# Four portions of x matmuls in place of five, in a graph aggregation kernel on one core

## What is computed

```python
def _L0_gnn_ref(feat_src, review_feat, edge_w, node_w, review_w, src_idx, dst_idx):
    h = feat_src @ node_w.T
    rf = review_feat @ review_w.T
    m = (h[src_idx] + rf) * edge_w
    return jax.ops.segment_sum(m, dst_idx, num_segments=N_DST)
x = _layernorm(x + _L0_gnn_ref(x, edge_attr_64, edge_weight1, ...), axis=-1)
```

## Time and profile before

| | us |
|---|---|
| median of 2 runs | 2188.48 |
| lowest, highest | 2188.12, 2188.84 |
| the profiled execution's own time | 2191.23 |
| its span, first to last instruction | 2189.4 |
| TensorE / VectorE / ScalarE / GpSimd busy | 1842.9 / 1854.2 / 1432.4 / 1582.9 |

### The profile page before, as it was taken

One profiled execution on the slowest core, in us unless ns is written; L12 is line 12 of the kernel. 1 busy time (PEld: TensorE's weight loads), 2 busy tenths in 40 slices (PEclk: granted clock), 3 DMA queues, 4 the chain that ended last, 5 costly groups with the idle time before them and its releaser, 6 DMA issues.

```text
span 2189.4 us, 95528 instructions
## 1 busy us (share of the span) xinstructions
PE 1842.9 (84%) x35999; PEld 1621.5 (74%) x36000; DVE 1854.2 (85%) x5664; ACT 1432.4 (65%) x2705; POOL 1582.9 (72%) x1539
## 2 busy tenths in 40 slices
PE   1669798979898989888898899889988997989984
PEld 1558687868787878777787788778877886878874
DVE  3859797979798989888898899789978897979974
ACT  1547675767676766766676667566766775767744
POOL 3777777777777777777777777777777777777501
PEclk8679898989999999989999999899989998989997
DMA  7223333333343333333333334333433343333302
GB/s 144 50 64 84 82 83 75 85 75 84 81 88 80 87 80 88 80 85 73 87 83 84 72 86 86 81 74 84 88 76 73 83 92 75 81 76 86 69 4 59
DMA packets 480122, 173.28 MB, mean 79 GB/s; under 512 B 443549, under 2 KB 455397, under 8 KB 479445
## 3 DMA queue, kind: packets, MB, share of 16 engines
q1 hardware_dynamic: 426791, 111.57, 23.8%
q0 software_dynamic: 49632, 51.95, 10.7%
q10 hardware_dynamic: 3218, 3.20, 0.7%
HBM read 163.39 MB, written 3.20 MB: 76 GB/s over the span
## 4 chain that ended last, share of the span: by engine, by line
POOL 63%; issue 20%; PE 7%; DVE 6%; DMA 2%; ACT 1%; DVEq 0%; POOLq 0%; ACTq 0%; SPq 0%
POOL rows L541 60%; PE x_ps L1493 3%; PE count_ps L1480 3%; POOL work L567 2%; DVE hot_lo L865 2%; DVE hot_key L864 1%; DMA counts<-dst 1%; POOL dst_row L559 1%; PE unit_ps L1405 1%; DMA dst_row<-dst,row_i 1%; ACT x_tab L1361 1%; DVE work L1000 0%; ACT counts L1283 0%; DVE x_tab L1020 0%; DVE x_tab L1008 0%
## 5 line engine op out<-in xcount | busy, mean ns | idle before, releaser
L541 POOL DMA_INDIRECT rows<-x,g_src_cols x1440 | 1496.1, 1039 | 443.4 <-issue 438.4
L1283 ACT ACTIVATE counts<-count_ps 128x588 f32<-128x588 f32 (+1 forms) x1192 | 836.0, 746 | 617.5 <-PE count_ps L1480 615.0
L1480 PE MATMUL count_ps<-hot_key,hot_lo 128*128 128x294 f32 x4552 | 863.5, 325 | 242.3 <-DVE hot_lo L865 177.4
L865 DVE SCALAR_TENSOR_TENSOR hot_lo<-count,cols 128x256 fp32r<-128x256 f16 x2276 | 1051.8, 477 | 1.0
L1480 PEld LDWEIGHTS count_ps<-hot_key,hot_lo 128*128 128x128 f32 x4552 | 664.2, 195 | 347.3 <-issue 170.5
L1493 PE MATMUL x_ps<-counts,x_tab 128*64 128x63 f32 x21364 | 789.7, 227 | 19.4 <-DVE sums L779 18.4
L1493 PEld LDWEIGHTS x_ps<-counts,x_tab 128*64 128x64 f32 x21364 | 715.7, 140 | 77.0 <-issue 26.1
L864 DVE TENSOR_SCALAR hot_key<-count,cols 128x294 fp32r<-128x294 f16 x1734 | 668.0, 385 | 71.7 <-PE count_ps L1480 60.1
L1240 ACT ACTIVATE hot_key<-far_key,all_ones 128x294 fp32r<-128x294 f16 x542 | 293.6, 542 | 17.6
L1238 ACT ACTIVATE far_key<-count,neg_key 128x294 f16<-128x294 f16 x542 | 284.7, 525 | 0.1
L1405 PE MATMUL unit_ps<-rows,g_hot 128*32 128x64 f32 x5760 | 120.1, 245 | 0.0
(11 more groups left out here) (199 smaller groups left out, 768.5 us busy)
## 6 DMA issues: line engine op xcount, KB each, us to landing
rows<-edge_attr SPq DMA_DIRECT2D x196, 512.0 KB
rows<-x,g_src_cols POOLq DMA_INDIRECT x1440
out<-x_tab SPq DMA_DIRECT2D x12, 256.0 KB
counts<-dst SPq DMA_DIRECT2D x1, 848.0 KB
a_stage<-dst SPq DMA_DIRECT2D x17, 48.0 KB
a_stage_w<-edge_weight SPq DMA_DIRECT2D x17, 48.0 KB
g_stage<-src SPq DMA_DIRECT2D x18, 40.0 KB
g_stage<-dst SPq DMA_DIRECT2D x18, 40.0 KB
```

The lines of the kernel that those rows point to most:

```text
L541: pool.indirect_dma_start(out=g_x[:, i, t, :], out_offset=None, in_=x, in_offset=bass.IndirectOffsetOnAxis(ap=g_src_cols[at.p][:, k:k + 1] ...
L865: dve.scalar_tensor_tensor(hot_lo[h][:, :, :], count16[:, 0:P].unsqueeze(1).to_broadcast([P, 2, P]), cols_[:, LO, j:j + 1], cols_[:, W_LOW ...
L1283: act.activation(to, count_ps[(g + e) % 2][:, 0:n, 0:KEYS].rearrange("p a (h d) -> p a h d", d=D), ACT.Copy).then_inc(counts_read, 1)
L1480: done = pe.matmul(count_ps[(g + e) % 2][:, k % 2, 0:KEYS], hot_lo[h][:, i, :], hot_key[h][:, :], start=(i == 0), stop=(i == 1))
```

## The change

The constants place four portions at k = 5, 10, 15 and 20 instead of five at 4, 8, 12, 16 and 20. The portions hold 24, 25, 24 and 25 x matmuls (before: 19, 20, 19, 20 and 20). The sums and products of the units move with them. On VectorE three positions move: `add_g` with the next `make_g_slot_hot` from 15 to 16, `make_a_hot` from 18 to 21, and `add_a` with the next `make_a_slot_hot` from 24 to 26. `make_g_hot` stays at 9. No instruction is added or removed, and ScalarE's, GpSimd's and SyncE's orders stay as they are.

```diff
-PORTIONS_AT = (4, 8, 12, 16, 20)
-SUM_G, MULTIPLY_G, SUM_A, MULTIPLY_A, TURN = 4, 8, 12, 16, 8
+PORTIONS_AT = (5, 10, 15, 20)
+SUM_G, MULTIPLY_G, SUM_A, MULTIPLY_A, TURN = 5, 10, 15, 20, 8
...
-                        if k == 15 and has_g:
+                        if k == 16 and has_g:
                             add_g(at, g)
                             if later_g:
                                 make_g_slot_hot(*next_unit(at, g, GATHERED))
-                        if k == 18 and later_a:
+                        if k == 21 and later_a:
                             make_a_hot(*next_unit(at, g, SUMMED))
                         if k == 22 and g == 1 and not last:
                             find_runs(at.r + 1)
-                        if k == 24 and has_a:
+                        if k == 26 and has_a:
                             add_a(at, g)
```

## The result

The changed kernel takes 2214.76 us (2213.83 to 2215.70, two runs) against 2188.48: the ratio is 1.011, with a 95% interval of 1.009 to 1.014. That is slower, by 26.3 us, and within the 2% that count as the same here. The forecast was 2198.5, in a range of 2189 to 2226: 10 us more were expected, 26 came, so the time lies in the range and 16 us above its centre. The profiled executions took 2191.23 and 2213.83 us and so differ by 22.6; the rest lies in how each stands to its median. Spans are 2189.4 and 2212.1.

What follows compares the result with a forecast made beforehand. GpSimd's 84 gathers, 113.2 us a round, were taken as the bound; two rounds of steps, 224.5 us, fit its 226.4, so 16 rounds cost nothing. The end adds 10 us: 2188.5 to 2198.5 us, range 2189 to 2226.

Steps and rivals of the forecast that it cites:

- What bounds: GpSimd, going from gather to gather without a stop, sets the period for 16 rounds: 84 gathers, 113.2 us a round.
- Five windows in a row: Between portions, a third pair waits for the first pair's evacuation: 0.45 us at windows 8, 14 and 18, 1.35 a step.
- Window 4: TensorE waits there for ScalarE's evacuation of windows 0 and 1, delayed by keys: 1.19 us a step.
- The plain step: TensorE's own work of 15.35 us plus waits of 1.35 and 1.19: 17.9 us, 2.1 more than before.
- The 16 rounds: Two rounds of steps, 224.5 us, still fit GpSimd's 226.4; line 809's wait falls from 134 to 50 to 80 us.
- Rival B: Steps outgrow GpSimd, over about 18.2 us on average; line 809's wait vanishes; 2230 us at 18.6 plain; chance 0.16.
- The end: Behind the last row transfer, nine and a half steps at TensorE's and VectorE's pace cost 1.2 us each: 10 us.
- The 16 rounds cost nothing: GpSimd's row transfers stay 113.2 us apart and the longer steps fit, so these rounds add 0 us.
- Queues: SyncE's attribute loads and GpSimd's gathers wait for sum_g about 1 us later in a step; cost taken as nothing.
- Rival A: Hidden anyway: ScalarE idles 34 of 135 us, so its copies may be in time; 2187 to 2190 us; chance 0.12.
- Rival C: TensorE's pauses lower the granted clock, 12 to 24 us a round; 2400 us and more; chance 0.03.
- The rule weighed: Independent matmul groups rotating through PSUM banks overlap evacuations, so two pairs suffice and nothing is lost: 2188 us.

Runs made afterwards that it cites:

- half copy: Changed kernel in which ScalarE copies only half of the counts in each evacuation behind the first group: 2208.11 us, 1.0082 of the kernel before.
- portions alone: Kernel before with only the portions moved to 5, 10, 15 and 20, sums, products and VectorE's positions left in place: 2192.73 us, ratio 1.0018.
- small loads: Kernel before with SyncE's attribute loads fetching 128 rows, not 2,048, behind four full loads: 2189.85 us, ratio 1.0003.

## Why the prediction came out as it did

- **What bounds: right.** GpSimd still waits for issue only, 438.7 us, and the chain is still 82% GpSimd and its issue.
- **Five windows in a row: right.** 0.45 us at windows 8, 14 and 18 was forecast, reckoned from starts. The rows show 0.40 to 0.41 of idle there, and in starts 0.53, 0.49 and 0.53 (2002.86 − 2001.37 − 0.96 for the last). In all 160.0 us of waits for ScalarE were measured, "over 150" was said. The half copy takes most of them away.
- **Window 4: right in place, a little off in size.** 0.84 us of idle, in starts from window 20 on 2008.27 − 2005.45 − 1.6 (five windows of 0.32) = 1.2, and 1.19 was forecast.
- **The plain step: 17.9 forecast, 18.1 to 18.35 measured.** With the waits in starts its own sum gives 15.35 + 1.55 + 1.22 = 18.1.
- **The 16 rounds: still fit, as said.** Line 809 waits for 55.8 us, in the 50 to 80 that were given, and by turns nothing and 3.0 to 3.5 us (3.7 the last time), as forecast. Rival B's sign, its row gone, did not come.
- **The end: 10 forecast, 10.5 measured.**
- **"The 16 rounds cost nothing": wrong, and this is the miss.** The step that failed is the one that took GpSimd's round as a constant, 113.2 us, because its instructions and their number stay. It is 113.94; up to the last find_runs that is 12.2 us, and with the end's 10.5 the 22.7 between the spans. Of the 0.76 us for a round, 0.63 are the longer gathers: 11.3 us over 18 rounds. Counted over the fourteen rounds alone, gathers take 0.70 us a round more, and 0.44 of that is in those held behind `prepare_g` and `prepare_a`: four more of them, and at other distances. The rest, 0.26, lies in gathers of 1.1 to 1.3 us, 193 where there were 138. What lengthens these was not tried. VectorE's `a_slot_hot` (line 751), which the change moves from position 24 to 26, also takes longer, 0.51 us in the median where it took 0.29; whether the two belong together is not shown. That the time came out inside the range owes something to luck: the range was drawn for late evacuations and for steps that outgrow GpSimd, and the longer gathers were in neither. A better reading of the trace of before would have seen gathers from 0.94 to 3.1 us in one and the same line, and asked what the long ones stand beside, before it took their mean as a price.
- **Queues: one thing overlooked.** `take_src` for unit 0 stands at position 14 of step 1, and the gather of that unit waits for it. Before, this was in time; after, three gathers of these fourteen rounds (597.39, 825.93 and 1737.25) begin 0.4 us late, 0.09 us a round. The profile names no releaser for them; the same gathers are among those that wait for `take_src` by name where the prepare instructions are left out. It is small here, but with quicker gathers it becomes the bound (27.4 us above, of which 5.0 stand at the start in every kernel). The prediction named only SyncE's loads, `sum_g` and find_runs.
- **Rival A is out:** the copies are not in time. **Rival C is out:** in the window below the granted clock is 1.00 in the end's steps, the upper level of 2.4 GHz, and over the whole span it rose, from 0.924 to 0.947, which fits the shorter stops at find_runs. With pauses of 0.4 to 0.85 us, four in 18 us, no fall is seen. The loss that the Trainium skill (TensorE: Matmul & The Clock Gate, psum-queue depth-cycling) describes for short pauses between groups in PSUM does not show at this size of pause.
- **The rule weighed** (the Trainium skill, Perfetto Trace Analysis, Matmuls) gave 2188 by itself. The rows were right to overrule it: here a pair fills 0.64 us, and its neighbour's copy with both hand-overs needs 1.09.
- **Small slips in its arithmetic.** Its terms for two rounds add up to 224.2, not 224.5; its upper bound for a step, with 0.2 us more at each of four releases, to 2.9 us, not 3.2; rival B's two rounds at 18.6 to 222.6, not 222.3. None changes the forecast.

The window of the changed kernel (stretch, its length, busy us of PE, PEld, DVE, ACT and POOL, granted clock, DMA share, GB/s):

```profile
1984.00:2119.00 135.00, 119.45 (x2463) 103.74 (x2464) 124.76 (x386) 94.86 (x177) 71.51 (x72) 1.00 0.29 61
```

TensorE is busy for 119.45 us of 135 where it was 128.21 in the earlier trace rows: 8.8 us more of pauses in a stretch of the same length.

**What stays open.** The mechanism by which a gather is held behind these VectorE instructions, and which of them does it, was not tried. That the relative position of the two engines' work decides is read from the single gathers: at 0.14 to 0.51 and at 0.92 to 1.26 us behind the last instruction's start they are held; in fourteen cases, in the kernel before and in those with portions alone and with small loads, they begin 0.60 to 0.62 us behind it and none is held. Also each change of pace or order gave another sum (1496 to 1515 us). But no kernel shifted this position alone. Why the gathers of 1.1 to 1.3 us grow in number is open too.

## What to carry over

When work runs beside pieces that need each other's buffer, count what stands between two uses: here 4 windows and a portion hid a copy, 5 windows in a row did not, and the sum was right to 0.5 us for a step of 18. An engine whose instructions the change doesn't touch can still change its pace; where that engine is the bound, look at its single instructions, not only at their mean, and see what the slow ones stand beside. If they stand behind a cluster of another engine's instructions, spreading the cluster may be worth more than the change at hand.

## What the runs showed of the hardware

- A gather of 1 us took 2.0 to 3.1 when it began within about 1.1 us behind the four or three short prepare instructions of VectorE (80 or 96 partitions), and ended 3.25 us behind the start of the last of them; the four that began 0.61 us behind it took 1.1. With the same instructions spread out no gather of these rounds was over 1.7. That was worth 25 us.
- Cutting 512 KB attribute loads to 32 KB left the gathers as they were.
- An x matmul takes 0.063 us (12 in 0.76) where neighbours alternate between the two halves of the output. The 34 extra ones, 17 in a row on one half, took 0.11 us each: their portion lasts 2144.99 − 2139.89 = 5.10 us, and 1.32 without them. The 17 also share their operands and add into the same columns, so which of these costs the time is not separated. From the timeline of PE with 34 extra matmuls (two records are one matmul):

```profile
2139.89 0.92 PE L1494 MATMUL x_ps<-counts,x_tab 128*64 128x63 f32 x24
2140.65 1.97 PE L1500 MATMUL x_ps<-counts,x_tab 128*64 128x63 f32 x31
...
2142.51 2.03 PE L1500 MATMUL x_ps<-counts,x_tab 128*64 128x63 f32 x33
...
2144.99 1.36 PE L1481 MATMUL count_ps<-hot_key,hot_lo 128*128 128x294 f32 x8
```
